# Softmax attention on one core: q and k held as two 16-bit float halves, a score as one product of 48 rows and two shift rows

## What is computed

```
x   -> layernorm -> q, k, v = x Wq^T, x Wk^T, x Wv^T     (16 heads of 16 features)
q,k -> rotated by position (cos, sin)
out  = softmax(q k^T / 4) v, per head;   x + out Wo^T
```

## Time and profile before

| | |
|---|---|
| median of the runs | 2536.25 us |
| profiled execution | 2524.04 us, its span 2522.3 us |
| PE busy | 2337.0 us, 93% |
| DVE busy | 1695.4 us, 67% |
| ACT busy | 1320.5 us, 52% |
| POOL busy | 1150.6 us, 46% |
| projection, to 233.3 us | PE 217.83, POOL 198.52 us busy |
| mixing, 286.4 to 1048.5 us | PE 729.84, DVE 665.84 us busy |

### The profile page before, as it was taken

One profiled execution on the slowest core, in us unless ns is written; L12 is line 12 of the kernel. 1 busy time (PEld: TensorE's weight loads), 2 busy tenths in 40 slices (PEclk: granted clock), 3 DMA queues, 4 the chain that ended last, 5 costly groups with the idle time before them and its releaser, 6 DMA issues. The chain is left out here.

```text
span 2522.3 us, 50928 instructions
## 1 busy us (share of the span) xinstructions
PE 2337.0 (93%) x15846; PEld 1283.8 (51%) x15846; DVE 1695.4 (67%) x4309; ACT 1320.5 (52%) x2741; POOL 1150.6 (46%) x1495
## 2 busy tenths in 40 slices
PE   8997899999999999979998996999999969998997
PEld 5664233333333333346656764566666646655765
DVE  6777888888888888548663323677777757764322
ACT  5665576767776677745433323555555525432322
POOL 7997111111111111124326775777777734325776
PEclk9998799999999999989998998999999989998999
DMA  6655443424333333136767984011111025685886
GB/s 190 216 188 175 96 108 80 106 80 109 79 103 86 100 89 84 38 106 211 262 214 209 235 200 79 18 35 39 36 38 37 18 73 189 215 287 169 233 213 115
DMA packets 286874, 325.25 MB, mean 129 GB/s; under 512 B 30496, under 2 KB 272368, under 8 KB 286704
## 3 DMA queue, kind: packets, MB, share of 16 engines
q1 hardware_dynamic: 252928, 274.22, 36.3%
q0 software_dynamic: 29184, 46.43, 9.2%
q10 hardware_dynamic: 4592, 2.47, 0.4%
HBM read 217.29 MB, written 105.19 MB: 128 GB/s over the span
## 5 line engine op out<-in xcount | busy, mean ns | idle before, releaser
L720 DVE TENSOR_REDUCE a_row_max<-a_ps_m 128x1 f32<-128x512 f32 x1024 | 637.5, 682 | 45.8 <-PE a_ps_m L619 42.3
L780 ACT ACTIVATE a_probs<-a_ps_s 128x512 f32<-128x512 f32 x1024 | 528.5, 603 | 253.0 <-PE a_ps_s L648 253.0
L665 PE MATMUL a_ps_o<-a_probs,a_va 128*32 128x512 f32 x2048 | 273.0, 606 | 0.2 <-ACT a_o_sb L789 0.2
L1760 POOL TENSOR_TENSOR b_spread<-b_decay,held_own_sb 128x512 f32<-128x512 f32 x256 | 267.7, 1077 | 8.6 <-DVE b_weight L1821 8.6
L1821 DVE TENSOR_TENSOR b_weight<-b_ps_s,b_spread 128x512 f32<-128x512 f32 x256 | 163.7, 681 | 9.4 <-PE b_ps_s L1962 9.4
L597 POOL DMA_DIRECT2D x<-a_xo x32 | 24.2, 755 | 264.7 <-DVE a_row_max L720 225.8
L558 POOL CAST a_high<-a_row_max 128x32 bf16<-128x32 f32 x32 | 6.5, 204 | 298.6 <-DVE a_row_max L720 298.6
L648 PE MATMUL a_ps_s<-first_qs,first_ks 48*128 48x512 bf16 (+1 forms) x1024 | 137.7, 388 | 5.3 <-DMA first_qs<-a_m_parts 3.8
L648 PE MATMUL a_ps_s<-second 48*128 48x512 bf16 (+1 forms) x1024 | 132.9, 377 | 4.3 <-DMA second<-a_m_parts 2.5
L619 PE MATMUL a_ps_m<-first_ks,first_qs 48*128 48x512 bf16 x512 | 106.9, 414 | 28.9 <-DVE a_row_max L720 27.4
L318 PE MATMUL a_ps_qk<-a_w_qk,a_xnT 128*128 128x512 f32 x256 | 121.4, 597 | 0.0
(11 more groups left out here) (395 smaller groups left out, 5385.5 us busy)
## 6 DMA issues: line engine op xcount, KB each, us to landing
parts<-second SPq DMA_DIRECT2D x16, 1536.0 KB, 6.3
second<-parts SPq DMA_DIRECT2D x384, 64.0 KB, 2.5
rows<-m_early SPq DMA_DIRECT2D x32, 640.0 KB, 4.1
m_early<-x SPq DMA_DIRECT2D x31, 512.0 KB, 4.1
first_qs<-parts SPq DMA_DIRECT2D x192, 64.0 KB, 2.9
first_ks<-parts SPq DMA_DIRECT2D x192, 64.0 KB, 2.3
m_own<-in_L_ffn_w_gate_dram SPq DMA_DIRECT2D x24, 384.0 KB, 4.4
m_own<-in_L_ffn_w_up_dram SPq DMA_DIRECT2D x24, 384.0 KB, 5.2
```

The lines of the kernel that those rows point to most:

```text
L665: last = nc.tensor.matmul(ps_o[VW * j:VW * (j + 1), :], va[n.u][:, t, (h0 + j) * VW:(h0 + j + 1) * VW], probs[:, group % 2, j, t, :], star ...
L720: nc.vector.tensor_reduce(row_max[:, n.k // 4 % 2, t, e, n.p % 4:n.p % 4 + 1], m_bank(name, step)[:], AX.X, ALU.max).then_inc(m_drained, 1)
L780: nc.scalar.activation(probs[:, group % 2, j, t, :], s_bank(name, step)[:], ACT.Exp, scale=DK ** -0.5).then_inc(s_drained, 1)
L1760: nc.gpsimd.tensor_tensor(spread[:, n % 2, heads].rearrange("p h t c -> p (h t) c"), decay[:, n % 3, heads].rearrange("p h (t o) -> p (h t ...
```

## The change

The parts become fp16 and two halves: high, and 64 times the rest. A third stored part is high / 64. The rows of q are (high, 64 rest, high / 64), those of k (high, high / 64, 64 rest), so one product of 48 rows gives high·high + rest·high + high·rest. Layer 1 goes; the shift rows join the one layer, and `scores` issues one matmul for a head and key tile in place of two. `max_products` still takes 48 rows, of the new parts. The loads of a sequence are 24 in place of 48. In the projection POOL's `split` becomes `scale_high` with lag 6, and the rows of -1 of set 0 are written at its start, by POOL and DVE.

```diff
-Q_PARTS = (0, 0, 1, 1, 0, 2)
-K_PARTS = (0, 1, 0, 1, 2, 0)
+Q_PARTS = (0, 1, 2)
+K_PARTS = (0, 2, 1)
...
+            nc.gpsimd.memset(const["first_ks"][EDGE + FILL_ROW:2 * EDGE, :, :], -1.0).then_inc(rows_set, 1)
+            pool.wait_ge(rows_set, 2)
...
-            def split(n, k):
+            def scale_high(n, k):
                 j, u = k % TPB, k % 2
-                pool.wait_ge(mid_done, n + 1)
-                nc.gpsimd.tensor_tensor(parts[:, k // TPB, 2, :, j * P:(j + 1) * P], rest[:, u, :].rearrange("p (g t) -> p g t", g=4), parts[:, k // TPB, 1, :, j * P:(j + 1) * P],
-                                        ALU.subtract).then_inc(low_done, 1)
+                pool.wait_ge(high_done, n + 1)
+                nc.gpsimd.tensor_tensor(parts[:, k // TPB, 2, :, j * P:(j + 1) * P], parts[:, k // TPB, 0, :, j * P:(j + 1) * P],
+                                        high_scale[:].rearrange("p (o t) -> p o t", o=1).to_broadcast([P, 4, P]), ALU.mult).then_inc(scaled_done, 1)
...
+            nc.vector.memset(const["first_ks"][FILL_ROW:EDGE, :, :], -1.0).then_inc(rows_set, 1)
...
-                wait(dve, low_done, n - 1)
+                wait(dve, mid_done, n - 1)
...
-                        pe.wait_ge(rest_loaded[u][f], 16 * 4 * (len(Q_PARTS) - MAX_SLOTS) * (n.base + n.k // PERIOD + 1))
-                        pe.wait_ge(rows_set[u], 2)
...
-                    for layer, shift_rows in ((0, 0), (1, 2)):
-                        for e in range(2):
-                            rows = slice(EDGE * e, EDGE * e + PART_ROWS + shift_rows)
-                            last = nc.tensor.matmul(s_bank(names[e], step)[:], ks[u][rows, n.p, layer, t * P:(t + 1) * P], qs[u][rows, n.p, layer, :],
-                                                    start=layer == 0, stop=layer == 1)
-                            if layer == 1:
-                                last.then_inc(s_filled, 1)
+                    for e in range(2):
+                        rows = slice(EDGE * e, EDGE * e + PART_ROWS + SHIFT_ROWS)
+                        nc.tensor.matmul(s_bank(names[e], step)[:], ks[u][rows, n.p, t * P:(t + 1) * P], qs[u][rows, n.p, :],
+                                         start=True, stop=True).then_inc(s_filled, 1)
```

More of the change, by code:

```diff
@@ L46, in turns, with operands @@
     return n // trip if isinstance(n, int) else (n - k) // trip
-Q_PARTS = (0, 0, 1, 1, 0, 2)
-K_PARTS = (0, 1, 0, 1, 2, 0)
-MAX_SLOTS = 3
-LAYERS = 2
+Q_PARTS = (0, 1, 2)
+K_PARTS = (0, 2, 1)
+SLOTS = 3
+REST_SCALE = 64.0
 EDGE = 64
-def operands(parts, q, k, b, f, slots):
+def operands(parts, q, k, b, f):
     for tile, parts_of, half in ((q, Q_PARTS, 0), (k, K_PARTS, 2)):
-        for slot in slots:
+        for slot in range(SLOTS):
             src = parts[b, 4 * parts_of[slot] + half + f].rearrange("(g e d) t -> e d g t", e=2, d=16)
             for e in range(2):
[L64 to L70, removed]
+                row = EDGE * e + slot * 16
+                yield tile[row:row + 16, f * 4:(f + 1) * 4, :], src[e]
 def attention_project(nc, dram, x_in, wq, wk, wv, const, ahead):
@@ L82, in attention_project @@
     TPB, TRIP = 4, 8
+    FILL_ROW = 32
     S = TPB * P
@@ L168, in load_first @@
                     sp.wait_ge(parts_stored[0], 16)
-                    for to, source in first_operands(dram["parts"], const["first_qs"], const["first_ks"], 0, n // 2 - 2):
+                    sp.wait_ge(rows_set, 2)
+                    for to, source in operands(dram["parts"], const["first_qs"], const["first_ks"], 0, n // 2 - 2):
                         sp.dma_start(to, source).then_inc(first_in, 16)
@@ L286, in middle @@
                 act.wait_ge(rest_done, n + 1)
-                nc.scalar.activation(parts[:, k // TPB, 1, :, j * P:(j + 1) * P], rest[:, u, :].rearrange("p (g t) -> p g t", g=4), ACT.Copy).then_inc(mid_done, 1)
+                nc.scalar.activation(parts[:, k // TPB, 1, :, j * P:(j + 1) * P], rest[:, u, :].rearrange("p (g t) -> p g t", g=4), ACT.Copy,
+                                     scale=REST_SCALE).then_inc(mid_done, 1)
             walk(act, TILES, TRIP, TRIP, [(1, normalise), (7, middle), (2, evacuate_x), (3, evacuate_v), (5, high)])
@@ L340, in attention_mix @@
     from contextlib import ExitStack
-    fp32, bf16 = mybir.dt.float32, mybir.dt.bfloat16
+    fp32, fp16 = mybir.dt.float32, mybir.dt.float16
     ALU, ACT, AX = mybir.AluOpType, mybir.ActivationFunctionType, mybir.AxisListType
@@ L393, in attention_mix @@
         row_max = sb("row_max", [P, 2, QT, 2, 4])
-        high = sb("high", [P, QT, 2, 4], bf16)
+        high = sb("high", [P, QT, 2, 4], fp16)
         high_low = sb("high_low", [P, QT, 2, 2, 4])
-        m_parts = sb("m_parts", [2 * HALF, 2, S], bf16)
+        m_parts = sb("m_parts", [2 * HALF, 2, S], fp16)
         probs = sb("probs", [P, 2, 4, QT, S])
@@ L475, in _, with load_qk @@
         def _(sp):
-            def load_qk(b, u, f, slots, loaded):
-                for to, source in operands(dram["parts"], qs[u], ks[u], b, f, slots):
-                    sp.dma_start(to, source).then_inc(loaded[u][f], 16)
+            def load_qk(b, u, f):
+                for to, source in operands(dram["parts"], qs[u], ks[u], b, f):
+                    sp.dma_start(to, source).then_inc(first_loaded[u][f], 16)
             def scores_read(seq, f):
@@ L2062, in program @@
     from contextlib import ExitStack
-    fp32, bf16, u32 = mybir.dt.float32, mybir.dt.bfloat16, mybir.dt.uint32
+    fp32, fp16, u32 = mybir.dt.float32, mybir.dt.float16, mybir.dt.uint32
     P, D, T, E, SEQS, S = 128, 256, 8192, 64, 16, 512
@@ L2070, in scratch @@
         return nc.dram_tensor(name, shape, dt).ap()
-    split = {"parts": scratch("parts", (SEQS, 12, P, S), bf16), "v": scratch("v", (T, D))}
+    split = {"parts": scratch("parts", (SEQS, 12, P, S), fp16), "v": scratch("v", (T, D))}
     routed = {"rows": scratch("rows", (T + SPARE, D + E))}
@@ L2104, in program @@
         ahead_x = landing["ahead_x"] = ctx.enter_context(nc.sbuf_tensor("ahead_x", [P, WD], fp32))
-        with (nc.sbuf_tensor("first_qs", [P, 8, LAYERS, S], bf16) as first_qs, nc.sbuf_tensor("first_ks", [P, 8, LAYERS, S], bf16) as first_ks,
-              nc.sbuf_tensor("second", [P, 2 * 16 * S], bf16) as second):
+        with (nc.sbuf_tensor("first_qs", [P, 8, S], fp16) as first_qs, nc.sbuf_tensor("first_ks", [P, 8, S], fp16) as first_ks,
+              nc.sbuf_tensor("second", [P, 2 * 24 * S], fp16) as second):
             attention = dict(held, **landing, first_qs=first_qs, first_ks=first_ks, second=second)
```

50 lines of the change are left out of this document (21 added, 29 removed).

## The result

The changed kernel ran at 2525.09 us (median of 5 runs, 2516.96 to 2529.61), the kernel before, measured beside it, at 2537.94 (5 runs, 2535.42 to 2541.17). The ratio is 0.9947 [0.9929, 0.9964]: 13.4 us faster, between 9 and 18. The forecast was 2528 us from a difference of -8.1; the range, 2518 to 2537, holds the time.

The account below looks back on a forecast made before the run. The prediction took DVE's chain of maxima, with PE in lockstep, to bound the steady part, and PE the projection. Terms 3 + 3.6 + 1.2 + 0.3 = 8.1 us off the median 2536.25 gave 2528 us, range 2518 to 2537.

Parts of the forecast that it names:

- The bound: Steady part: DVE's chain, 1.17 us from max to max, hides the scores; PE needs 1.10 and has 0.07 to spare.
- Steady part: Steady mixing: plain half steps gain nothing, late-starting score products give back 3 us; bounds 0 and 8.
- Ramp: Start of mixing at clock 0.50: max to max falls from 2.10 to DVE's 1.42 us; net 3.6 saved, bounds 2 and 5.
- The half microsecond set aside for a later clock: Start of mixing: a less busy PE may get its faster clock up to a half step later; 0.5 us off the gain.
- Projection: Projection stage: POOL's new instruction costs nothing, PE stays the bound; one POOL instruction less at the end saves 0.3 us.
- POOL has 7.51 / 30 = 0.25 us a tile to spare: Projection: POOL's missing busy time was taken as slack, so its new instruction may take 1.41 us before it counts.
- Rival D: Projection: POOL becomes the bound with the multiplication at 1.6 us, +13, net +5, 2541 us; chance 0.06.
- Tail: End of mixing, after the last max product: ACT's 7 waits for score products shorten, 1.2 us saved; bounds 0 and 3.
- Loads and the writes of -1: Half the loads gone: 0, bounds 0 and -2; writes moved to the projection's start: 0, under 1 us if DVE is slow.
- A: Steady part: PE was the bound after all, DVE's gaps of at most 92.8 us close, about 2440 us; chance 0.05.
- B: Only the ramp gains; late starts move to another wait, ACT paces the tail; 2533 us, like no change; chance 0.11.
- C: Steady part: PE's pauses drop the clock to 0.50, a tenth of half steps cold, net +23, 2559 us; chance 0.09.

Follow-up runs that it names:

- experiment 3: The kernel before with the first layer's product left out of every score; parts, loads and projection unchanged: 2530.19 us, ratio 0.9962.
- experiment 5: The kernel before with DVE's row maxima taken over 256 of the 512 keys: 2478.28 us, ratio 0.9802.
- experiment 7: The changed kernel with POOL's multiplication a step later, behind the middle part, and DVE waiting for POOL again: 2513.94 us, ratio 0.9951.
- experiment 2: The changed kernel run again without any edit: 2525.74 us, ratio 0.9939.
- experiment 4: The changed kernel with every score product issued twice into the same bank, new parts, loads and projection kept: 2532.28 us, ratio 0.9967.
- experiments 9 and 10: Four banks for maxima, three for scores, scores spread evenly: in the changed kernel 2492.92 us (0.9876), in the kernel before 2598.95 us (1.0297).

## Why the prediction came out right, point by point

**The bound.** Right. PE at 96% was in lockstep with DVE: 90 us less of PE's work gave 3 us, and at most 5.6 (experiment 3), and experiment 5 shows the 1.10 us that the prediction had for PE's own need.

**Steady part.** Predicted -3, measured -3.0 (761.3, the mean of two, to 758.25). That the number fits is luck: two errors cancel. The gain was 5.6 us in experiment 3, and 5.4 in experiment 7, where nothing else disturbed it. It lies where the prediction looked for it, at the score products that start late: the half step from 644.58 us takes 3.41, its counterpart 3.07 in the changed kernel. The line that closes it before, and the two after:

```profile
647.99 0.39 PE L619 MATMUL a_ps_m<-first_ks,first_qs 48*128 48x512 bf16 x2
```

```profile
636.51 0.39 PE L612 MATMUL a_ps_m<-first_ks,first_qs 48*128 48x512 f16 x2
...
639.58 0.39 PE L612 MATMUL a_ps_m<-first_ks,first_qs 48*128 48x512 f16 x2
```

Such a half step comes once a sequence, and 15 x 0.34 is 5.1 us. The prediction had PE late by 0.35 there (646.10 against 645.75), but priced the place by DVE's idle time, 4.7 us in all, and took 3. Against the 5.4 to 5.6 stands a loss of 2.5 in both executions of the changed kernel, in the fourth and fifth sequence: some 1.6 us is the clock at 0.50 (experiment 2), the rest a wait for the shift rows of 1.20 and 1.37 us, 0.38 in experiment 7. The prediction had this at nothing. Why the rows came later there, and why the clock stayed up behind waits of 1.49 and 1.55 us in experiments 7 and 3, is open.

**Ramp.** Predicted -3.6, measured -4.4 to -4.7. The 1.39 us from max to max came as derived (1.42 forecast). The half microsecond set aside for a later clock was not needed, and neither was a term for loads (experiment 4).

**Projection.** Here a term was mis-sized: -0.3 (at most -1.2) forecast, -3.5 to -3.9 measured. The step that failed is "POOL has 7.51 / 30 = 0.25 us a tile to spare". What I divided were mostly the gaps between POOL's instructions (4.6 of the 7.51 us), not time in which it waited. The tiles of the kernel before stood 3.24 us apart at the start and mostly 3.30 from the fifth on, because POOL was the bound by 0.06 (in experiment 7, with the short instruction in the old place, they stand 3.24 apart where those of experiment 3, with the old one, stand 3.30); so 1.16 us already counted, and a shorter instruction won until 3.24, where POOL waits. Rival D had POOL at the bound too, but with the new instruction at 1.6 us; it took 1.04. The part of the term that I did price at 0.3, one POOL instruction less at the end, measured 1.4 us (8.92 to 7.50). The measured 3.5 to 3.9 is even too small: the two executions of the changed kernel started 1.0 to 1.4 us later than the kernel before, which experiments 9 and 10 show to be no part of the change.

My estimate from the Trainium skill's figure ("GPSIMD Engine Reference", section 3.1), 1.12 us, was near both rows: 1.16 before, 1.04 after. No harm came from it; harm came from the limit that I compared it with.

**Tail.** Predicted -1.2. Measured +1.2 and -1.2 against 48.05, the mean of the kernel before (49.3 and 46.9), and in experiments 3 and 7, which have one product too, +1.2 and +0.8. So the sign is not shown, and where the number fits it is luck. The step that failed is that each of ACT's waits shortens: they are 8.0 and 6.0 us against 6.9 and 6.2. PE, being earlier, waited 2.87 and 2.30 us for the shift rows in place of 1.8 and 1.1, and the clock fell in three of these four executions; the bounds (0 to 3) had no case for that.

**Loads and the writes of -1.** 0 forecast; experiment 4 bounds the loads at 1.2 us in the steady part, and DVE's first data came at 7.17 us with its write done at 5.24.

**The rivals.** A fell: no half step under 2.49 us while DVE reads 512 columns with three banks, and 104.6 us of PE's waits are named after DVE. B fell: timed runs tell 13 us from nothing, steady part and projection both gave something. C, the clock, came in a small part, and the prediction's own sign for it, a granted clock off 1.00 between 300 and 1040 us, did appear: 3.4 us at 0.50 in each execution, at a price of some 1.6 us, where C had a tenth of the half steps and +31. In the tail of one it cost another 2.4. What C named as its reason, the pauses before the max products, was not enough by itself: in 221 such waits, 104.6 us in all, the clock stayed at 1.00, and each fall stood behind a single longer wait for the shift rows (1.20, 1.51 and 2.87 us). Whether the pauses prepare it is open: with two score products a key tile, before and in experiment 4, waits for these rows of up to 1.8 us left the clock at 1.00. The Trainium skill's section "A second HAM failure mode: psum-queue depth-cycling" ("TensorE: Matmul & The Clock Gate") has the clock going back and forth with frequent short pauses between groups of products; this trace doesn't agree with that for pauses of 0.35 us in many of its half steps. D fell as told above.

**The sum.** 8.1 us forecast; by the stages 9.8 to 12.6, by the timed runs 13.4 [9, 18]. The projection gave 3.2 to 3.6 us more than its term and the ramp about 1; the tail took 2.4 back in one execution. The time itself was nearer (2525.09 to 2528) than the terms deserve, since both stand on a median that has its own scatter.

## What to carry to other kernels

A busy share doesn't name the bound: an engine at 96% lost 90 us of its work and the stage won 3, and one at 92% set the pace of another stage, because most of what it lacked were gaps between its instructions; so before a slack is computed from idle time, look in the timeline whether the engine waits for anybody. When work is taken from an engine that waits for another, look at once for an order that lets it run ahead: the same saving was worth 13 us in the old order, 41 with a lighter DVE and 106 in an order that had to carry it. And a stage total that fits the forecast can be two errors that cancel: compare the single half steps, and the granted clock in short windows, before calling a term right.

## What the runs showed of the hardware that was not expected

- DVE's maxima over 128x512 in PSUM, 683 ns each by the records, stand 0.62 us apart in lockstep with PE and 0.60 where products are ready ahead (sixteen in 9.64 us).
- POOL's multiplication of an fp16 128x512 by a broadcast f32 column takes 1032 to 1047 ns, against 1158 for a f32 minus bf16 and 1267 for a sum of two f32.
- The granted clock of TensorE fell to 0.50 for 3.4 us behind waits of 1.20 and 1.51 us, and did not behind waits of 1.37, 1.49 and 1.55 us elsewhere; in the tail it fell behind 2.87, 2.65 and 2.35 us and not behind 2.30. In the 221 waits for DVE, 104.6 us in all, it did not. A mean over a stage hides it: the steady part of the changed kernel reads 1.00.
- Executions of the same projection differ by up to 1.4 us in when PE's products get to full speed: two or four of the first ones with q and k take 1.06 us in place of 0.59.
- Two stages that gather and scatter rows by DMA varied by up to 12 us from one execution of the same kernel to the next, as much as the whole effect studied here.
